# A tile's accumulator folded on Pool in three additions in place of one reduce on VectorE

## What is computed

```
e = stack([tbl_j[ids[:, j]] for j in range(39)])          # (512, 39, 16)
X0, Xi = e, e
for W, b in ((W0, b0), (W1, b1), (W2, b2)):               # 128 outputs each
    Wr = W.reshape(128, 39, Fi)
    Xi = einsum('hjk,bjd,bkd->bhd', Wr, X0, Xi) + b[None, :, None]
    res.append(Xi.sum(axis=2))
h = concatenate(res + [dense_ctx], axis=1)
h = relu(h @ W_top1 + b_top1); h = relu(h @ W_top2 + b_top2); y = h @ W_top3
```

## Time and profile before

| | |
|---|---|
| median of 3 runs | 691.94 us (691.92 to 692.39) |
| the profiled execution | 694.63 us, its span 692.5 us |
| TensorE (PE) busy | 658.8 us, 95% |
| VectorE (DVE) busy | 593.3 us, 86% |
| ScalarE (ACT) busy | 560.8 us, 81% |
| Pool busy | 358.8 us, 52% |
| mean granted TensorE clock | 0.995 |

### The profile page before, as it was taken

The page is one execution under the profiler, slowest core; times in us unless marked ns, Lnnn a source line. Parts: engine busy times, 40 slices in busy tenths (PEclk is TensorE's granted clock), DMA queues, the critical chain, the costliest instruction groups (busy, mean ns, idle before and its releaser), DMA issues.

```text
span 692.5 us, 11925 instructions
## 1 busy us (share of the span) xinstructions
PE 658.8 (95%) x2662; PEld 475.0 (69%) x2662; DVE 593.3 (86%) x958; ACT 560.8 (81%) x1941; POOL 358.8 (52%) x394
## 2 busy tenths in 40 slices
PE   2788999999999999999999999999999999999898
PEld 2655777776767777677767676777667777767584
DVE  2557898999999998999999998999899999999870
ACT  2546889989888987988888887898799888899762
POOL 7734783746566464648383746557463415132700
PEclk9999999999999999999999999999999999999999
DMA  8216622314040504141322314050414140200000
GB/s 281 23 17 116 161 38 55 67 32 90 14 105 8 112 8 109 13 104 17 95 27 63 57 38 80 16 103 8 109 12 107 11 101 7 64 19 1 1 1 0
DMA packets 67394, 39.65 MB, mean 57 GB/s; under 512 B 58646, under 2 KB 61718, under 8 KB 65204
## 3 DMA queue, kind: packets, MB, share of 16 engines
q1 hardware_dynamic: 60463, 37.71, 24.4%
q0 software_dynamic: 5120, 1.29, 2.2%
q10 hardware_dynamic: 1760, 0.15, 0.2%
HBM read 32.80 MB, written 2.40 MB: 51 GB/s over the span
## 4 chain that ended last, share of the span: by engine, by line
PE 77%; DVE 6%; ACT 6%; issue 6%; DMA 3%; ACTq 0%; SPq 0%; POOL 0%; DVEq 0%; POOLq 0%
PE yb L979 18%; PE yb L980 17%; PE yb L981 17%; PE p L945 13%; ACT yb L624 5%; PE pq L956 4%; DVE acc L803 4%; DMA gram<-in_L_rec_W_dram 2%; PE pq L910 1%; PE yb L1085 1%; PE yb L897 1%; DMA late<-x_scratch 1%; DVE yb L789 1%; PE p L1057 1%; PE p L1055 1%
## 5 line engine op out<-in xcount | busy, mean ns | idle before, releaser
L624 ACT ACTIVATE yb<-yb,x0t 128x128 f32<-128x128 f32 x1728 | 468.9, 383 | 78.4 <-PE yb L981 71.6
L803 DVE TENSOR_TENSOR acc<-acc,yb 128x512 f32<-128x512 f32 (+1 forms) x576 | 385.3, 669 | 40.6 <-ACT yb L624 9.3
L979 PE MATMUL yb<-w1h,x1h 128*128 128x512 f32 (+1 forms) x640 | 315.3, 493 | 8.4 <-DVE acc L803 5.7
L980 PE MATMUL yb<-w1l,x1h 128*128 128x512 f32 (+1 forms) x640 | 248.1, 388 | 0.0
L981 PE MATMUL yb<-w1h,x1l 128*128 128x512 f32 (+1 forms) x640 | 248.1, 388 | 0.0
L979 PEld LDWEIGHTS yb<-w1h,x1h 128*128 128x128 f32 x640 | 120.3, 188 | 90.0 <-DVE acc L803 60.0
L476 POOL TENSOR_TENSOR late<-late,x0r 117x512 f32<-117x512 f32 (+1 forms) x105 | 132.0, 1290 | 88.7 <-DMA late<-x_scratch 88.5
L422 POOL DMA_INDIRECT emb<-in_table_dram,idx x160 | 152.6, 954 | 43.0 <-issue 38.8
L980 PEld LDWEIGHTS yb<-w1l,x1h 128*128 128x128 f32 x640 | 121.0, 189 | 41.2 <-issue 24.9
L981 PEld LDWEIGHTS yb<-w1h,x1l 128*128 128x128 f32 x640 | 120.4, 188 | 24.8
L465 POOL TENSOR_TENSOR bdiag<-mask,x0t 128x312 f32<-128x312 f32 x64 | 45.4, 710 | 156.3 <-PE pq L956 153.0
(11 more groups left out here) (108 smaller groups left out, 317.1 us busy)
## 6 DMA issues: line engine op xcount, KB each, us to landing
late<-x_scratch SPq DMA_DIRECT2D x45, 312.0 KB
late<-x_scratch SPq DMA_DIRECT2D x30, 234.0 KB
emb<-in_table_dram,idx POOLq DMA_INDIRECT x160
gram<-in_L_rec_W_dram SPq DMA_DIRECT2D x1, 2496.0 KB, 12.2
x_scratch<-x0r SPq DMA_DIRECT2D x15, 156.0 KB
late<-x_scratch SPq DMA_DIRECT2D x15, 156.0 KB
w2t<-in_L_rec_W_dram SPq DMA_DIRECT2D x1, 1280.0 KB, 15.6
x0t<-embt SPq DMA_DIRECT2D x64, 20.0 KB
```

What stands on the lines that cost most here:

```text
L624: op = act.activation(part, part, ACT.Copy, scale=x0t[u][:, t, j:j + 1])
L803: dve.tensor_tensor(part, part, parts(y_bank(t, m), n), ALU.add).then_inc(summed, 1)
L979: pe.matmul(y[:, 0:w], hi, w1h[:, at:at + w], start=True, stop=False)
L980: pe.matmul(y[:, 0:w], hi, w1l[:, at:at + w], start=False, stop=False)
```

## The change

VectorE's `tensor_reduce` of a tile is gone, and the accumulator has four slots in place of five. Pool computes the same in three additions: slots 0, 1 plus slots 2, 3 (128 x 2 elements, into `halves`), then the two halves (128 elements, into `whole`), then the bias `b1c` (128 elements, into `x2`). Each waits for the one before, on a new semaphore `folded`; the first waits for all nine sums of the tile, the third for the gram product that last read the x2 buffer.

On Pool's queue the fold of tile T - 1 stands ahead of the spread of tile T. At a seam, in the last tile of a group, a second fold stands behind the spread and ahead of the four early pair chunks: it is that of the group's last tile, whose sum of bank 9 VectorE makes within the next group's first tile. ScalarE's two copies of the bias into acc go.

```
-PARTS = BANK_F + 1
-DVE_ORDER = (..., ("sum", 1), ("sum", 2), ("fold before", 0), ("sum", 4), ...)
+DVE_ORDER = (..., ("sum", 1), ("sum", 2), ("sum", 4), ...)
-        acc = [sb(f"acc{u}", [P, HID, PARTS]) for u in range(2)]
+        acc = [sb(f"acc{u}", [P, HID, BANK_F]) for u in range(2)]
+        halves = [sb(f"halves{u}", [P, HID, 2]) for u in range(2)]
+        whole = [sb(f"whole{u}", [P, HID]) for u in range(2)]
...
 on Pool
+            pool.wait_ge(b1_in, 16)
             pool.wait_ge(embq_ready, 1)
...
+            def fold(T, p):
+
+                pool.wait_ge(summed, (T + 1) * N_SUM)
+                pool.tensor_tensor(halves[p][:, :, :], acc[p][:, :, 0:2], acc[p][:, :, 2:4], ALU.add).then_inc(folded, 1)
+                pool.wait_ge(folded, T * 2 + 1)
+                pool.tensor_tensor(whole[p][:, :], halves[p][:, :, 0], halves[p][:, :, 1], ALU.add).then_inc(folded, 1)
+                if at_least(T, 2):
+                    pool.wait_ge(gram_done, T - 1)
+                pool.wait_ge(folded, T * 2 + 2)
+                pool.tensor_tensor(x2[p][:, :], whole[p][:, :], b1c[:, :], ALU.add).then_inc(x2_ready, 1)
+
             def period(g, u, after):
                 for t in range(TILES):
+                    if t > 0:
+                        fold(g * TILES + t - 1, (t + 1) % 2)
                     if t == 0 and after > 2:
                         pool.wait_ge(embq_ready, g + 2)
                         rows_of(g + 3, 1 - u)
...
                     spread(g, t, u)
...
                     if t == 0 and after > 0:
                         for c in range(EARLY, CHUNKS):
                             pair_chunk(g + 1, c)
+                    if t == TILES - 1:
+                        fold(g * TILES + t, t % 2)
                     if t == TILES - 1 and after > 1:
                         for c in range(EARLY):
                             pair_chunk(g + 2, c)
...
             for t in range(TILES):
+                if t > 0:
+                    fold((GROUPS - 1) * TILES + t - 1, (t + 1) % 2)
                 spread(GROUPS - 1, t, 1)
                 split_dense(t)
+            fold(NT - 1, 1)
...
 on ScalarE
-            act.wait_ge(b1_in, 16)
-            for u in range(2):
-                act.activation(acc[u][:, :, BANK_F], b1c[:, :], ACT.Copy).then_inc(bias_ready, 1)
...
 on VectorE
-            def fold(T, t):
-                dve.wait_ge(summed, (T + 1) * N_SUM)
-                if at_least(T, 2):
-                    dve.wait_ge(gram_done, T - 1)
-                dve.tensor_reduce(x2[t % 2][:, :], acc[t % 2][:, :, :], AX.X, ALU.add).then_inc(x2_ready, 1)
...
-            dve.wait_ge(bias_ready, 4)
+            dve.wait_ge(bias_ready, 2)
...
-            fold(NT - 1, TILES - 1)
```

More of the change, by code:

```diff
@@ L53 @@
 RING = ACT_RING + DVE_RING
-PARTS = BANK_F + 1
-DVE_ORDER = (("sum before", 8), ("scale", 0), ("sum before", 9), ("scale", 3), ("sum", 1), ("sum", 2),
-             ("fold before", 0), ("sum", 4), ("sum", 3), ("scale", 6), ("sum", 5), ("sum", 7), ("sum", 6))
+DVE_ORDER = (("sum before", 8), ("scale", 0), ("sum before", 9), ("scale", 3), ("sum", 1), ("sum", 2), ("sum", 4), ("sum", 3), ("scale", 6), ("sum", 5), ("sum", 7), ("sum", 6))
 SUM_ORDER = (1, 2, 4, 3, 5, 7, 6, 8, 9)
@@ L225, in tower @@
         summed = sem("summed")
+        folded = sem("folded")
         x2_ready = sem("x2_ready")
@@ L819, in period @@
                         elif at_least(T, 1):
[L820 to L823, removed]
+                            add_bank(T - 1, (t + TILES - 1) % TILES, m)
                         if more and t == TILES - 1 and (kind, m) == ("sum", LOW_AT):
```

## The result

The changed kernel takes 752.12 us (median of 4 runs, 750.89 to 753.07) against 692.16 (691.92 to 693.86) for the kernel before on the same chip: ratio 1.0867, interval 1.0845 to 1.0889. It is slower by 60 us where 33 were forecast, and above the range. The profiled execution took 752.39 us, its span 750.6.

What follows compares the result with a forecast made beforehand. The prediction took TensorE to bound the kernel, with 77% of the chain. Seams +28.8, start-up +5.2, last group -3.5, tail +1.3 and +1.9, less 0.3, gave +33.4 us: 691.94 becomes 725.3 us, range 712 to 743.

Steps and rivals of the forecast that it cites:

- What bounds the kernel: Whole kernel: TensorE has 77% of the chain; its work is 35.2 us of each 37.1 us group.
- the most that a faster VectorE can give back: In the loop: TensorE loses only 1.9 us a group that a faster VectorE could return.
- Rival (b): In the loop: VectorE's relief wins, half of the 1.9 us a group gained, 685 us; chance 0.05.
- Price of a fold: On Pool, each tile: three dependent additions of 0.68, 0.43 and 0.43 us plus gaps, 2.05 us.
- rival (a): On Pool: strided reads make the three additions dearer, up to 3.2 us a tile, 741 us; chance 0.13.
- F of 3.2: On Pool: upper bound in us for one tile's three additions, with strided reads doubling the part above fixed cost.
- The seam's stall: At 14 seams: chunk 0 starts at +7.6 where TensorE arrives at +3.95, a stall of 3.65 us.
- rival (c): At the seam: VectorE isn't earlier, its last sum still ends at +4.8, 736 us; chance 0.12.
- signs of being wrong: In the changed profile: chunk 0 under +6, an addition under 0.3 or over 1 us, or TensorE's waits for VectorE's sums remaining.
- part 3: At the seams: Pool's fold ahead of the early pairs stalls TensorE; groups take 39.1 us, +28.8 us in all.
- Start-up: In group 0: tile 0's fold comes behind Pool's late pairs, so TensorE's gram(0) slips by 5.2 us.
- Last group and tail: After the loop: last group -3.5 us; last fold on Pool +1.3 and Pool's splits slowing VectorE +1.9.

Runs made afterwards that it cites:

- the wait alone: Kernel before, with only a wait of Pool for the bank-9 sum of the group's last tile ahead of the early pairs: 706.59 us against 692.65, ratio 1.0200.
- no folds: Changed kernel without Pool's additions or any fold, x2 holding zeros, gram products waiting for the sums: 686.52 us against 692.65, ratio 0.9908.
- the first experiment: Changed kernel with Pool making the four early pair chunks before the fold of the group's last tile: 698.11 us against 692.65, ratio 1.0083.

## Why the prediction was wrong, point by point

**What bounds the kernel: mostly right, one term mis-sized.** No run has a group under the 35.2 us of TensorE's work. But "the most that a faster VectorE can give back" was put at 1.9 us a group. Without any fold it is 37.04 - 36.69 = 0.35. Of the rest some 0.9 a group goes with ScalarE's hole ((37.9 - 35.8) in five groups of twelve), which I took into the mean of 37.1 without asking who made it; 0.6, by which the best odd groups (35.83) stay above 35.2, isn't assigned. For the forecast this didn't matter. Rival (b) took half of the 1.9, 0.95 a group, where the whole relief is worth 0.35.

**Price of a fold: right.** Forecast 0.68, 0.43 and 0.43 with gaps of 0.25; the rows after show these means:

```profile
L486 POOL TENSOR_TENSOR halves<-acc 128x256 f32<-128x256 f32 x64 | 39.2, 613 | 182.3 <-DVE acc L822 181.6
L492 POOL TENSOR_TENSOR x<-whole,b1c 128x128 f32<-128x128 f32 x64 | 29.3, 458 | 5.9
...
L488 POOL TENSOR_TENSOR whole<-halves 128x128 f32<-128x128 f32 x64 | 25.6, 401 | 5.0
```

1.47 us and gaps under 0.1 (421.73 to 421.81). The strided additions are no dearer than the dense third one (0.401 against 0.458 for 128 elements), and rival (a) falls. Its F of 3.2 was slightly off in itself: its own terms, 2 x (1.54 - 0.6) + 0.6 + 0.6, give 3.1.

From the 4497 ns for 2048 elements of the page GPSIMD Engine Reference of the Trainium skill (section Performance versus the Vector engine) the estimate was 1.1 us without fixed parts; measured are 1.47.

**The seam's stall: right where the clock stays up, in part by luck.** Forecast: chunk 0 at +7.6, sum's end at +4.05, groups of 39.1. Measured: +7.44, +4.46, and 38.88 and 39.08 in groups 2 and 8. Two errors of 0.4 cancel, the fold cheaper, the sum later: of VectorE's 0.72 only 0.35 arrive at the seam, so rival (c) was half right. The idle time itself is 3.00 and not 3.65, since TensorE comes at +4.4 and not at +3.95. One of my signs of being wrong came true: TensorE's waits for VectorE's sums remain, 35.2 us of the 60.0 of the kernel before.

**The step that failed** is in part 3: "a group becomes 35.2 + 3.65 + 0.2 left over". It takes each matmul behind the stall at the price of one without a stall. After 3 us of idleness TensorE works at its lower level, and chunk 0, three banks and more cost 5.83 us in place of 4.23. This comes at twelve of the fourteen seams: 12 x 1.6 = 19 us, nearly all of the 21 by which groups 1 to 14 exceed the forecast. The run with the scratch addition has the same low clock without any fold on Pool, and the one with TensorE busy has chunk 0 as late without the low clock. I had the mean granted clock of the kernel before in the table, 0.995, and priced nothing by it. The trace of the kernel before had a case to read the term from: in group 0 TensorE stands 2.76 us for chunk 0's pair, and in the 6 us behind it the clock is 0.72 and the matmuls start 0.43 apart (columns of the last row as above: TensorE's busy time, clock, DMA).

```profile
62.05 1.10 PE L945 MATMUL p<-late,w0t 117*128 117x512 f32 x2 [2.76 <-POOL late L476]
...
64.32 0.63 PE L980 MATMUL yb<-w1l,x1h 128*128 128x512 f32 x1
64.75 0.63 PE L981 MATMUL yb<-w1h,x1l 128*128 128x512 f32 x1
```

The clock there, from the windows:

```profile
62.00:68.00 6.00, 5.95 (x16) 0.72 0.39 40
```

**Start-up: mechanism right, size short.** 7.7 us and not 5.2: TensorE stood 4.66 us at gram(0), and the 9 us behind it show a granted clock of 0.75, which is a quarter of 9, 2.3 us, lost. It is the same missing term, and moving the folds gives the 7.7 back (48.53 to 40.83).

**Last group and tail.** -2.3 and not -3.5. Without any fold the group still takes 36.03 against 36.20, so of the missing 1.2 us at most 0.2 are Pool's, and no engine waits for Pool in it. ScalarE idles only 1.3 us for TensorE's banks in these 36 us, so it is near its own limit; I didn't separate it from VectorE. The tail, +3.7 against +3.2, is as told; 2.8 of it come back with the fold on VectorE.

**The range.** It took in two dearer mechanisms of Pool and none of TensorE. Its upper end of 743 lies just above the 741 of a fold of 3.2 us at 14 seams, while no seam was asked what else a longer stall does.

## What to carry to other kernels

Before work is put into another engine's queue, ask of every wait that comes with it who stands behind it in that queue and how much slack he has: here a slack of 2.2 us met a pair that is ready 4.8 later (+7.4 in place of +2.6), and swapping two blocks gave back 54 of 60 us. Price a new stall of TensorE as its length and the slower matmuls behind it as well: behind idle times of 2.3 and 3.0 us they cost 1.6 us more at most of the seams here. Look for a case in the trace of before; this one had it in group 0. And before saving time on an engine, divide the idle time of the bounding engine by who makes it: 0.35 us a group were VectorE's, not 1.9.

## What the runs showed of the hardware

- Idle times of TensorE ahead of chunk 0, and the clock behind them, in groups 2 to 13 of one run each: 1.48 us, no fall in any; 2.33 to 2.36, a fall in eight; 3.00, a fall in ten; 0.38 after 2.78 us of useless transposes, none.
- Nearly equal idle times, 2.33 and 2.36 at consecutive seams, end in both ways, so the idle time alone doesn't decide. Elsewhere it is the same: in group 0, 2.76 us (kernel before) are followed by 0.72, but 2.56 (the wait alone) and 3.12 (no folds) by 1.00; and 1.57 us ahead of the last gram of the first experiment are followed by 0.72 in the 6 us from 643 on. What else decides wasn't looked into.
- While the clock is low a 128x512 matmul starts 0.42 to 0.43 us behind the one before; at the full clock 0.23.
- Pool's additions read fp32 with strides of two and four elements at no more than the price of a dense one: 0.613 us for 256 elements and 0.401 for 128, against 0.458 for the dense third of 128.
- The two subtractions of SBUF operands on VectorE (L870) take 3.47 us for two while Pool runs its splits, against 1.28 without Pool beside them; Pool's splits take 1.67 each then, in place of 1.46.
